# Two transformer layers with routed experts: how VectorE picks the experts, rewritten around its eight-largest instruction

## The reference

```
# layer 0: best two of eight, weights renormalised
g = softmax(h @ Wr); top2_w, top2_idx = top_k(g, 2)
top2_w = top2_w / sum(top2_w)
out = sum over the two of top2_w * (relu(h @ W1[e]) @ W2[e])
# layer 1: best one of eight, weighted by its softmax score
scores = softmax(xn @ gate_w.T); top1_idx = argmax(scores)
out = max(scores) * (silu(xn @ W1[e] + b1[e]) @ W2[e] + b2[e])   for e = top1_idx
```

## Time and profile before

| | us |
|---|---|
| median of 3 runs | 2274.51 (2273.72 to 2276.03) |
| the profiled execution's own time | 2273.52 |
| its span in the trace | 2271.7 |
| attention stage of layer 0, from DVE's first statistics to POOL's last scatter | 55 to 827 |
| experts stage of layer 0 | 832 to 1143 |
| attention stage of layer 1, in the same way | 1171 to 2009 |
| experts stage of layer 1 | 2018 to 2272 |

### The profile page before, as it was taken

The page is one execution under the profiler, slowest core; times in us unless marked ns, Lnnn a source line. Parts: engine busy times, 40 slices in busy tenths (PEclk is TensorE's granted clock), DMA queues, the critical chain, the costliest instruction groups (busy, mean ns, idle before and its releaser), DMA issues. The chain is left out here.

```text
span 2271.7 us, 57921 instructions
## 1 busy us (share of the span) xinstructions
PE 1787.5 (79%) x15650; PEld 1288.8 (57%) x15650; DVE 1694.5 (75%) x5861; ACT 1039.5 (46%) x1967; POOL 951.4 (42%) x1028
## 2 busy tenths in 40 slices
PE   1699999999999929999906777777777777719997
PEld 1466666666667618999803444444444444407776
DVE  3488888888888746666627988998999899824453
ACT  0266666666666612222204555555555555602322
POOL 0233444343444324454425455445545554313433
PEclk7699999999999969999957999999999998959999
DMA  3334444444444332222235443544444444343332
GB/s 125 48 69 70 75 74 76 70 76 71 75 73 73 61 72 59 71 69 67 60 115 90 100 98 91 98 101 100 94 99 98 96 96 95 70 141 96 100 92 62
DMA packets 260822, 191.15 MB, mean 84 GB/s; under 512 B 24824, under 2 KB 251002, under 8 KB 260046
## 3 DMA queue, kind: packets, MB, share of 16 engines
q1 hardware_dynamic: 245402, 155.40, 33.2%
q0 software_dynamic: 15360, 35.03, 5.4%
HBM read 95.37 MB, written 53.15 MB: 65 GB/s over the span
## 5 line engine op out<-in xcount | busy, mean ns | idle before, releaser
L849 DVE TENSOR_REDUCE mx<-A 128x2 f32<-128x512 f32 x1024 | 692.6, 683 | 127.5 <-PE A L1097 51.1
L701 ACT ACTIVATE probs<-B 128x1024 f32<-128x1024 f32 x512 | 524.0, 1023 | 350.4 <-PE B L1120 180.8
L1093 PE MATMUL A<-stack 126*128 126x256 bf16 x2048 | 440.7, 287 | 159.6 <-DVE mx L849 127.9
L1117 PE MATMUL B<-stack 128*128 128x256 bf16 x2048 | 364.1, 281 | 31.8 <-DMA stack<-mrow 31.6
L1093 PEld LDWEIGHTS A<-stack 126*128 126x128 bf16 x2048 | 180.8, 100 | 328.9 <-DVE mx L849 244.4
L1132 PE MATMUL M<-probs,vals 128*32 128x256 f32 x4096 | 289.1, 399 | 21.6 <-DVE On L875 17.4
L611 POOL DMA_INDIRECT gathered<-h,slot_in x192 | 187.2, 975 | 155.2 <-DVE slot_in L988 109.6
L1117 PEld LDWEIGHTS B<-stack 128*128 128x128 bf16 x2048 | 203.4, 103 | 83.2 <-issue 31.2
L598 POOL TENSOR_TENSOR h<-xn,back_rows 128x256 f32<-128x256 f32 x64 | 46.4, 724 | 465.6 <-DVE xn L803 465.6
L1533 PE MATMUL A<-w2s,hid 128*128 128x128 f32 x1792 | 230.5, 279 | 9.0 <-issue 9.0
L1533 PEld LDWEIGHTS A<-w2s,hid 128*128 128x128 f32 x1792 | 211.9, 192 | 18.3 <-issue 13.3
(11 more groups left out here) (193 smaller groups left out, 3079.2 us busy)
## 6 DMA issues: line engine op xcount, KB each, us to landing
stack<-parts SPq DMA_DIRECT2D x768, 64.0 KB
xt<-gathered SPq DMA_DIRECT2D x112, 132.0 KB, 2.2
back_rows<-mod_rows SPq DMA_DIRECT2D x64, 192.0 KB, 3.4
probs<-gathered SPq DMA_DIRECT2D x40, 256.0 KB, 2.7
w<-in_w SPq DMA_DIRECT2D x4, 2048.0 KB
Y<-expert_out SPq DMA_DIRECT2D x64, 128.0 KB
front_rows<-mod_rows SPq DMA_DIRECT2D x32, 192.0 KB
X<-in_x SPq DMA_DIRECT2D x32, 128.0 KB, 3.2
```

The lines of the kernel that those rows point to most:

```text
L701: act.activation(probs[c % 4][:, :, :, :], Bp[c % 2][:, :, :, :], ACT.Exp, scale=EXP_SCALE[l][c // 4]).then_inc(b_exp.handle, 1)
L849: dve.tensor_reduce(mx[u][:, h, :], A[h % 2][:, :, :], AX.X, ALU.max).then_inc(a_max.handle, 1)
L1093: ins = pe.matmul(A[h % 2][:, t, :], stack[u][0:n, h, 0, t * P:(t + 1) * P], stack[u][0:n, h, 1, :], start=True, stop=(l == 1))
L1117: ins = pe.matmul(Bp[c % 2][:, j, t, :], stack[u][:, h, 1, t * P:(t + 1) * P], stack[u][:, h, 0, :], start=True, stop=(l == 1))
```

## The change

`first_of`, `choose_first` and `choose_second` go. Two steps take their place. `rank` calls `dve.max` for each of the two token tiles, which returns the eight logits in descending order, and `dve.max_index`, which returns where each stands; it also takes the difference for the weights. `choose` copies the index of the best expert into the row (so the row now carries the index `FIRST` and not the reversed index `REV`) and compares both choices with a row of expert numbers in one instruction (`chosen`, 32 elements a partition; layer 1 writes `sel` at once). `place` multiplies both one-hot rows in one instruction and reduces with a maximum straight into the integer slots. In layer 0 `rank` stands where `choose_first` stood, `choose` where `choose_second` stood; in layer 1 both stand where `choose_first` stood.

```diff
-            def first_of(src, top, eq, cand, idx, dst):
-                ch.link(dve.tensor_reduce(top, src, AX.X, ALU.max))
-                ch.link(dve.tensor_tensor(eq, src, top.unsqueeze(2).broadcast_to([P, NT, E]), ALU.is_equal))
-                ch.link(dve.tensor_tensor(cand, eq, rev_iota[:, :, :], ALU.mult))
-                ch.link(dve.tensor_reduce(idx, cand, AX.X, ALU.max))
-                ch.link(dve.tensor_tensor(dst, rev_iota[:, :, :], idx.unsqueeze(2).broadcast_to([P, NT, E]),
-                                          ALU.is_equal))
...
-            def choose_first(b, k, u):
+            def rank(b, k, u):
                 row = (h3 if l else h2)[u]
                 dve.wait_ge(scattered.handle, scattered.after(b - 2))
+                dve.wait_ge(logits_read.handle, logits_read.after(b))
                 ch.mark(dve.tensor_scalar(row[:, :, TOKEN], token_ids[:, bass.ds(b, 1), :].rearrange("p o t -> p (o t)"),
                                           1.0, None, ALU.mult))
-                dve.wait_ge(logits_read.handle, logits_read.after(b))
-                first_of(lg[:, :, :], r1[:, 0, :], rt[:, 0, :, :], rt[:, 1, :, :], row[:, :, REV], rt[:, 2, :, :])
+                for t in range(NT):
+                    ch.mark(dve.max(best[:, t, :], lg[:, t, :]))
+                ch.settle_apart()
+                for t in range(NT):
+                    ch.mark(dve.max_index(best_at[:, t, :], best[:, t, :], lg[:, t, :]))
+                if l:
+                    dve.tensor_tensor(less[:, :, :], lg[:, :, :], best[:, :, 0:1].broadcast_to([P, NT, E]),
+                                      ALU.subtract).then_inc(w_den.handle, 1)
+                else:
+                    dve.tensor_tensor(less[:, :, 0], best[:, :, 1], best[:, :, 0], ALU.subtract).then_inc(w_den.handle, 1)
+                ch.settle()
+
+            def choose(b, k, u):
+                row = (h3 if l else h2)[u]
+                ch.mark(dve.tensor_copy(row[:, :, FIRST], best_at[:, :, 0]))
                 if l:
                     dve.wait_ge(pos.handle, pos.after(b - 1))
-                    dve.tensor_copy(sel[:, :, :], rt[:, 2, :, :]).then_inc(sel_ready.handle, 1)
...
+                    dve.tensor_tensor(sel[:, :, :], expert_ids[:, :, 0, :], best_at[:, :, 0:1].broadcast_to([P, NT, E]),
+                                      ALU.is_equal).then_inc(sel_ready.handle, 1)
+                else:
+                    ch.link(dve.tensor_tensor(chosen[:, :, :, :], expert_ids[:, :, :, :],
+                                              best_at[:, :, 0:2].unsqueeze(3).broadcast_to([P, NT, 2, E]), ALU.is_equal))
+                    dve.wait_ge(pos.handle, pos.after(b - 1))
+                    dve.tensor_tensor(sel[:, :, :], chosen[:, :, 0, :], chosen[:, :, 1, :], ALU.add)\
+                        .then_inc(sel_ready.handle, 1)
...
             def place(b, k, u):
...
-                for c in range(n_choice):
-                    ch.link(dve.tensor_tensor(rt[:, 6 + c, :, :], rt[:, 2 + 2 * c, :, :], rt[:, 5, :, :], ALU.mult))
-                for c in range(n_choice):
-                    ch.mark(dve.tensor_reduce(r1[:, 8 + c, :], rt[:, 6 + c, :, :], AX.X, ALU.add))
-                ch.settle()
+                if l:
+                    dve.wait_ge(sel_ready.handle, sel_ready.after(b))
+                    ch.link(dve.tensor_tensor(placed[:, :, 0, :], sel[:, :, :], place_of[:, :, :], ALU.mult))
+                else:
+                    ch.link(dve.tensor_tensor(placed[:, :, :, :], chosen[:, :, :, :],
+                                              place_of[:, :, :].unsqueeze(2).broadcast_to([P, NT, 2, E]), ALU.mult))
                 dve.wait_ge(pos_read.handle, pos_read.after(b))
-                dve.tensor_copy(slot_in[u][:, 0:n_choice, :], r1[:, 8:8 + n_choice, :]).then_inc(slots_ready.handle, 1)
+                dve.tensor_reduce(slot_in[u][:, 0:n_choice, :].rearrange("p c t -> p t c"), placed[:, :, 0:n_choice, :],
+                                  AX.X, ALU.max).then_inc(slots_ready.handle, 1)
...
-                layer(0, choose_first, -3)
+                layer(0, rank, -3)
...
-                layer(0, choose_second, -3)
-                layer(1, choose_first, -3)
+                layer(1, rank, -3)
+                step(choose, -3)
```

More of the change, by code:

```diff
@@ L23 @@
 PADS = E + TAIL
-TOKEN, REV, W0, W1 = range(D, D + 4)
+TOKEN, FIRST, W0, W1 = range(D, D + 4)
 W = D + 4
@@ L213, in build @@
         lg = sb("lg", [P, NT, E])
-        rt = sb("rt", [P, 8, NT, E])
-        r1 = sb("r1", [P, 16, NT])
+        best = sb("best", [P, NT, E])
+        best_at = sb("best_at", [P, NT, E], mybir.dt.uint32)
+        chosen = sb("chosen", [P, NT, 2, E])
+        place_of = sb("place_of", [P, NT, E])
+        placed = sb("placed", [P, NT, 2, E])
+        less = sb("less", [P, NT, E])
+        less_exp = sb("less_exp", [P, NT, E])
+        den = sb("den", [P, NT])
         sel = sb("sel", [P, NT, E], BF16)
@@ L394, in attention @@
     (X, XR, X1, st, mv, rs, xn, hT, qk, rem, parts, stack, vals, mx, mneg, mrow, probs, heads, rsum, On, OnT, yT,
-     st2, mv2, rs2, xn2, front_rows, back_rows, xh, qs_bias, h2, h3, h2T, eps_col, lg, rt, r1, sel, slot_in, token_ids, run) = (g[n] for n in (
+     st2, mv2, rs2, xn2, front_rows, back_rows, xh, qs_bias, h2, h3, h2T, eps_col, lg, best, best_at, chosen, place_of, placed, less, less_exp, den,
+     sel, slot_in, token_ids, run) = (g[n] for n in (
         "X XR X1 st mv rs xn hT qk rem parts stack vals mx mneg mrow probs heads rsum On OnT yT "
-        "st2 mv2 rs2 xn2 front_rows back_rows xh qs_bias h2 h3 h2T eps_col lg rt r1 sel slot_in token_ids run").split())
+        "st2 mv2 rs2 xn2 front_rows back_rows xh qs_bias h2 h3 h2T eps_col lg best best_at "
+        "chosen place_of placed less less_exp den sel slot_in token_ids run").split())
     A, Bp, M0, M1, M0b, ident, ident_b, slope_ident, dist = (g[n] for n in
@@ L401, in attention @@
         "wq wk wv wo qk_bias q_scale modT gob gate_w ln_cols".split())
-    before_tri, ones_b, rev_iota, mod_rows, gathered, x_view, region_row = (g[n] for n in
-        "before_tri ones_b rev_iota mod_rows gathered x_view region_row".split())
+    before_tri, ones_b, expert_ids, mod_rows, gathered, x_view, region_row = (g[n] for n in
+        "before_tri ones_b expert_ids mod_rows gathered x_view region_row".split())
     gb_row, ones_col, lnrow, Y, expert_out, XR, a, w1, w2, b1, b2 = (g[n] for n in
@@ L728, in weights @@
                 if l:
-                    act.activation(rt[:, 4, :, :], rt[:, 3, :, :], ACT.Exp).then_inc(w_exp.handle, 1)
+                    act.activation(less_exp[:, :, :], less[:, :, :], ACT.Exp).then_inc(w_exp.handle, 1)
                 else:
-                    act.activation(r1[:, 5, :], r1[:, 4, :], ACT.Exp).then_inc(w_exp.handle, 1)
+                    act.activation(less_exp[:, :, 0], less[:, :, 0], ACT.Exp).then_inc(w_exp.handle, 1)
             def tick(at):
@@ L953, in choose_second @@
-            def choose_second(b, k, u):
-                ch.link(dve.scalar_tensor_tensor(out=rt[:, 3, :, :], in0=rt[:, 2, :, :], scalar=-BIG, in1=lg[:, :, :],
-                                                 op0=ALU.mult, op1=ALU.add))
-                first_of(rt[:, 3, :, :], r1[:, 2, :], rt[:, 0, :, :], rt[:, 1, :, :], r1[:, 3, :], rt[:, 4, :, :])
-                dve.wait_ge(pos.handle, pos.after(b - 1))
-                dve.tensor_tensor(sel[:, :, :], rt[:, 2, :, :], rt[:, 4, :, :], ALU.add).then_inc(sel_ready.handle, 1)
-                dve.tensor_tensor(r1[:, 4, :], r1[:, 2, :], r1[:, 0, :], ALU.subtract).then_inc(w_den.handle, 1)
+                    dve.tensor_tensor(sel[:, :, :], expert_ids[:, :, 0, :], best_at[:, :, 0:1].broadcast_to([P, NT, E]),
[6 more added lines that the diff above has]
+                        .then_inc(sel_ready.handle, 1)
@@ L964, in weigh_choices @@
                 if l:
-                    ch.link(dve.tensor_reduce(r1[:, 6, :], rt[:, 4, :, :], AX.X, ALU.add))
-                    ch.mark(dve.reciprocal(row[:, :, W0], r1[:, 6, :]))
-                else:
-                    ch.link(dve.tensor_scalar(r1[:, 6, :], r1[:, 5, :], 1.0, None, ALU.add))
-                    ch.link(dve.reciprocal(row[:, :, W0], r1[:, 6, :]))
-                    ch.mark(dve.tensor_tensor(row[:, :, W1], r1[:, 5, :], row[:, :, W0], ALU.mult))
+                    ch.link(dve.tensor_reduce(den[:, :], less_exp[:, :, :], AX.X, ALU.add))
+                    ch.mark(dve.reciprocal(row[:, :, W0], den[:, :]))
+                else:
+                    ch.link(dve.tensor_scalar(den[:, :], less_exp[:, :, 0], 1.0, None, ALU.add))
+                    ch.link(dve.reciprocal(row[:, :, W0], den[:, :]))
+                    ch.mark(dve.tensor_tensor(row[:, :, W1], less_exp[:, :, 0], row[:, :, W0], ALU.mult))
             def place(b, k, u):
@@ L1594, in inputs_of @@
         "before_tri": bits(r < c), "ones_b": bits(np.ones((P, P))),
[L1595 removed]
```

(1 more changed line is left out.)

23 lines of the change are left out of this document (10 added, 13 removed).

## The result

The changed kernel takes 2318.1 us (median of 4 runs, 2315.4 to 2319.3), the kernel before 2274.95 on the same chip (4 runs, 2273.7 to 2276.0): 1.019 times as long, interval 1.017 to 1.021. The forecast was 2251. The profiled execution took 2317.5 us, with a span of 2315.7.

What follows compares the result with a forecast made beforehand. Bound: in layer 0 a DVE, POOL and SP loop of some 45.0 us per two ticks, in layer 1 a loop through DVE's update. 14.3 + 8.9 = 23.2 us off 2273.5 gives 2250.3, as median 2251; range 2237 to 2267.

Steps and rivals of the forecast that it cites:

- the likeliest case: Whole kernel: the forecast of 2251 us itself, own range 2242 to 2262, chance 0.5.
- Rank and choose in layer 1: DVE between heads 9 and 11: 1.14 us falls to 0.86, 0.28 saved a tick, 8.1 us over 29 full ticks.
- The rival of slow searches: Searches at the upper bound: layer 1 loses 0.41 us a tick, 12 us, total 2272, halfway 2262; chance 0.2.
- The first and second choice in layer 0: DVE's choice steps: the residual can move only to yT's end, so 0.46 us a tick reaches the loop.
- the 2.1 at the end: Layer 0's three last ticks, engines nearly empty: serial choice once and `place` twice save 2.1 us.
- Place in layer 0: DVE's `place` falls from 1.07 to 0.6 us; 0.47 saved a tick, counting in full on the path.
- the loop: Layer 0: DVE's `second_norm`, POOL's `modulate`, scatter and split, SP's parts, head 0; some 45.0 us is two ticks.
- 8.74 us from split to head 0: Layer 0: constant distance from POOL's split end to head 0, meaning the split parts' transfer releases head 0 every time.
- Its two halves: Layer 0's loop: `modulate` to head 0 of the next tick but one, 22.81 us; head 0 to `modulate`, 22.59.
- PE as the bound: Layer 0: POOL's round trip shortens too, ticks fall to 21.4 us, total 2236; chance 0.15.
- Hidden in layer 0: Head 0 waits for something else at once; only layer 1 and the tails count, total 2263; chance 0.1.
- Slower through held searches: Searches held like DVE's L932, or simply slow: kernel slower from 0.32 us a search, 2294 at 0.5; chance 0.05.

Runs made afterwards that it cites:

- e9: Changed kernel with 100 memsets on DVE ahead of layer 1's loop, tiles still 32 bytes past multiples of 64 (e5's kernel, another chip): 2256.87 us, 0.992 of before.
- e1: Changed kernel with 100 memsets on DVE ahead of layer 1's loop, whose 400-byte tile also put later tiles at multiples of 64 bytes: 2244.74 us.
- e2: Changed kernel with 256 memsets on DVE ahead of layer 1's loop: 2317.7 us.
- e3: Kernel before, without the change, with 202 memsets on DVE ahead of layer 1's loop: 2329.7 us.
- e15: Changed kernel with 196 memsets on DVE ahead of layer 1's loop: 2253.4 us.
- e11: e9 with two more linked 0.2 us steps in layer 0's `place`, and 80 memsets to keep layer 1's loop body where it was: 2250.46 us.
- e14: Kernel before with only the change's `place` in layer 0, and 29 memsets to keep layer 1's loop body where it was: 2287.65 us, 1.0055 of before.
- e10: e9 with layer 0's wait for the scatter's landing moved behind the next q and k split on POOL (e7's kernel, e9's chip): 2248.4 us.
- e12: Kernel before with layer 0's wait for the scatter's landing moved behind the next split, on e9's chip: 2279.2 us, 1.001 of before.
- e4: e1 with two more linked 0.2 us steps in layer 0's `place`, which also moved layer 1's loop body: 2301.1 us.
- e16: e11 with its tiles at multiples of 64 bytes: 2240.15 us, 0.984 of the kernel before.
- e5: e1 with a 1024-byte memset tile, so later tiles lie 32 bytes past multiples of 64: 2367.3 us, 0.992 of before on that chip.
- e7: e5 with layer 0's wait for the scatter's landing moved behind the next q and k split on POOL: 2365.6 us.
- e8: Kernel before with layer 0's wait for the scatter's landing moved behind the next split, on e5's chip: 2386.9 us against 2388.2 before.

## Why the prediction was wrong

**The step that failed** is layer 1's: "**0.28 saved**. Over the 29 full ticks 8.1 us". It counts only what DVE executes. The loop body as a piece of code, which begins 52 instructions earlier and from there stops at each jump back, was in none of the steps or rivals. The stop is worth 61 us in all, about 5 a body (e9 against the changed kernel; that it comes from the place is shown by e1 to e3 and e15). Without it the forecast of 2251 stands against 2256.9 (e9), inside the likeliest case's own range of 2242 to 2262. That nearness is in part luck: layer 0 gave 5.5 us for 14.3 forecast, layer 1 12.9 for 8.9.

**Rank and choose in layer 1** were right in mechanism and a little under-sized: 0.36 us saved, not 0.28 (searches and sorts 0.43 from start to start, not 0.54). From head 0 to head 0 undisturbed ticks are 24.65 and 24.54 us (e9) for 25.02 and 25.06, 0.44 less on average, and layer 1 gained 12.9 us for the 8.9 forecast. The 0.08 a tick that ranking and choosing leave unexplained could be `place`, whose 0.2 us behind L980 I had put at nothing; that wasn't tried alone. From 1300 to 1900 us PE waited for that update 21.5 us in 24 times before and in e1, as forecast. The rival of slow searches is out.

**The first and second choice in layer 0** went as said: the residual stands right behind yT with DVE idle before it (14.0 us of such waits, 27 times). Two kernels that differ in the choices and hardly in `place` are before (layer 0 ends at 831.9) and e11 (820.1): 11.8 us, where the steps gave 0.23 x 26 = 6 and part of the 2.1 at the end. With the short `place` the choices are worth even more, 19.5 us (e14 against e9), so the price of one step depends on the other.

**Place in layer 0** takes 0.60 us as said:

```profile
469.14 0.16 DVE L988 TENSOR_TENSOR place_of<-M,run 128x16 f32<-128x16 f32 x1
...
469.64 0.18 DVE L999 TENSOR_REDUCE slot_in<-placed 128x4 int32<-128x32 f32 x1
469.74 0.69 DVE L857 TENSOR_REDUCE mx<-A 128x2 f32<-128x512 f32 x1
```

Its worth has the wrong sign. "0.47 saved ... it counts in full" should have given 6 us; e9 against e11 shows 6.4 lost, e14 against the kernel before 12 lost. The step took the loop for one in which every term is fixed but DVE's. The row on which it stood, 8.74 us from split to head 0, is itself not fixed (8.75 and 9.12 in turn after the change, up to 9.87 in e14, 10.1 to 11 in e10 and e12), nor is the landing. Its two halves were also of different parities: 22.81 and 22.59 add up to 45.40, not to the 44.99 of two ticks; the half that closes the loop with 22.59 is 22.40 (474.12 to 496.52). The split starts 9.5 us behind SP's issue of the second half's parts in one parity and 9.2 to 9.4 in the other (before, after, e9, e11), whenever the scatter came: 451.60 to 461.15 before, 449.63 to 459.17 after. That distance would explain most of what the round trip took back; that the scatter shares the engines with these transfers is my reading of it and was not tried alone.

**The rivals.** PE as the bound held for every second tick: no wait ahead of head 0 and 21.7 us, near the 21.4 worked out, but the other tick took 1.6 more. Hidden in layer 0 came nearest to what is seen there, for another reason than the one given. Slower through held searches: L954, the difference behind them, takes up to 1006 ns in layer 0 (448 in the median) while POOL splits, but the searches never took longer (153 to 172 ns).

## What to carry to other kernels

A change of an engine's code in front of or inside a loop of some 300 instructions can cost or save a stop at every jump back, whichever instructions they are: read the row of the instruction queue and the "issue" wait of the first instruction behind the jump, and shift the loop by idle instructions before the change itself is judged. Where several loops of a pipeline have nearly the same length, half of what is saved per tick is not a safe price for the loop that was found: lengthen the step by the same amount first and see whether the time follows.

## What was not expected of the hardware

- The stop at the jump: 2.6 to 3.4 us, twelve times, with five instruction packets of 8 KB each time; it depends on the body's place modulo 128 instructions (table above).
- Tiles at multiples of 64 bytes rather than 32 past one: SP's six stacking transfers are over 8.36 us behind the split instead of 8.74 (e4, e16 and every second tick of e1 against e2, e9, e11), and layer 0 is 6.4 to 7.4 us shorter.
- In the changed kernel a sort of eight from eight logits a partition takes 144 to 165 ns (up to 331 in e7) with 0.08 us from start to start, the load of the values to match 66 to 93 ns, the search 153 to 172 ns.
- On one of the four chips the same kernels ended layer 0 at 937 to 957 us instead of 821 to 837 (e5, e7, e8 against e9, e10, e12), with layer 1 unchanged (854.9 and 868.6). What was longer is the time until ACT gets PE's product with the values: 2.1 to 5.5 us after its start once in every tick, where 1.1 is usual. For the bytes they moved the transfers were no slower: the queue of SP's transfers was busy 26.7% of the 600 us for 31.5 MB in e5, 35.1% for 36.9 MB in e9.
- On the other chips the same product comes 0.7 to 1.4 us late once in two ticks of every kernel with the short `place` in layer 0 (seven runs). Neither is explained.
